# The last row of a hybrid layer stack made as two units of 256 tokens, with gate and output products in parts

## What is computed

```python
x = x + _L0_attn_a_ref(_layernorm(x), ...)   # mamba block
x = x + _L0_ffn_ref(_layernorm(x), ...)      # ternary FFN "a"
x = x + _L0_attn_b_ref(_layernorm(x), ...)   # minGRU
x = x + _L0_ffn_ref(_layernorm(x), ...)      # ternary FFN "d"
```

```python
def step(hstate, inp):
    dt_s, B_s, C_s, u_s = inp
    dA = jnp.exp(dt_s[..., None] * A)
    hstate = dA * hstate + (dt_s * u_s)[..., None] * B_s[:, None, :]
    y = jnp.einsum('bdn,bn->bd', hstate, C_s)
    return (hstate, y)
```

## Time and profile before

| | |
|---|---|
| median of three runs | 849.01 us (847.75 to 850.52) |
| the profiled execution | 847.88 us |
| its span in the trace | 846.1 us (1.8 us lie outside) |
| mean granted TensorE clock | 0.905 of full |
| first scan of row 0; of row 7 | 34.04 us; 645.91 us |
| end of the last scan step (row 7) | 731.9 us |
| from there to the end of the span | 114.2 us |

### The profile page before, as it was taken

One profiled execution on the slowest core, in us unless ns is written; L12 is line 12 of the kernel. 1 busy time (PEld: TensorE's weight loads), 2 busy tenths in 40 slices (PEclk: granted clock), 3 DMA queues, 4 the chain that ended last, 5 costly groups with the idle time before them and its releaser, 6 DMA issues. The chain is left out here.

```text
span 846.1 us, 12506 instructions
## 1 busy us (share of the span) xinstructions
PE 704.9 (83%) x4060; PEld 592.6 (70%) x4060; DVE 677.5 (80%) x1063; ACT 638.3 (75%) x965; POOL 586.3 (69%) x375
## 2 busy tenths in 40 slices
PE   5666576799689988899789979999789968988966
PEld 4454465588677876688667868688668857877765
DVE  4799988799977997999888998799879987743131
ACT  5787877896899878987999688987896588335312
POOL 3499768777768787978777887878796578225312
PEclk9678577999899997999899989999899989998995
DMA  5511211111111211121111211211112110000000
GB/s 140 175 62 63 76 51 54 48 64 51 38 51 52 63 38 58 44 72 42 52 45 56 63 39 52 63 51 48 53 32 71 50 51 26 0 1 2 13 1 12
DMA packets 35185, 42.79 MB, mean 51 GB/s; under 512 B 7457, under 2 KB 17074, under 8 KB 35122
## 3 DMA queue, kind: packets, MB, share of 16 engines
q1 hardware_dynamic: 35122, 42.00, 16.3%
HBM read 39.63 MB, written 2.36 MB: 50 GB/s over the span
## 5 line engine op out<-in xcount | busy, mean ns | idle before, releaser
L523 POOL TENSOR_TENSOR inflow<-dtu,b_all 128x1024 f32<-128x1024 f32 x127 | 308.9, 2435 | 72.3 <-DVE state L1127 45.9
L1127 DVE TENSOR_TENSOR_SCAN state<-dA,inflow 128x512 f32<-128x512 f32 x256 | 298.4, 1207 | 27.1 <-ACT dA L874 23.9
L874 ACT ACTIVATE dA<-dt,decay_c 128x512 f32<-128x512 f32 x256 | 170.1, 686 | 48.2 <-DVE state L1127 47.2
L1144 DVE TENSOR_TENSOR state<-state,c_ps 128x1024 f32<-128x1024 f32 x128 | 155.7, 1216 | 18.8 <-PE c_ps L1432 13.9
L1441 PE MATMUL y_ps<-ident,state 128*128 128x128 f32 x1024 | 149.9, 295 | 0.0
L1441 PEld LDWEIGHTS y_ps<-ident,state 128*128 128x128 f32 x1024 | 134.6, 154 | 13.8 <-issue 4.1
L1432 PE MATMUL c_ps<-xd,pick 128*128 128x512 f32 x128 | 64.2, 502 | 58.0 <-DVE state L1144 57.3
L1325 PE MATMUL work<-in_hi,wzh_hi 128*128 128x512 f32 x256 | 104.2, 407 | 2.3 <-POOL in_lo L685 2.2
L1326 PE MATMUL work<-in_hi,wzh_lo 128*128 128x512 f32 x256 | 101.0, 395 | 0.0
L1327 PE MATMUL work<-in_lo,wzh_hi 128*128 128x512 f32 x256 | 101.0, 394 | 0.0
L676 POOL TENSOR_TENSOR wide<-wide 128x512 f32<-128x512 f32 x48 | 61.2, 1274 | 29.0 <-ACT wide L921 26.8
(11 more groups left out here) (172 smaller groups left out, 1491.4 us busy)
## 6 DMA issues: line engine op xcount, KB each, us to landing
b_all<-b_scratch SPq DMA_DIRECT2D x128, 256.0 KB, 3.1
x_tok<-in_x SPq DMA_DIRECT2D x8, 256.0 KB, 3.8
out_x<-x_tok SPq DMA_DIRECT2D x8, 256.0 KB, 3.7
wide<-in_Wz SPq DMA_DIRECT2D x1, 1024.0 KB, 7.9
wide<-in_Wh SPq DMA_DIRECT2D x1, 1024.0 KB, 8.3
skip_f<-in_W SPq DMA_DIRECT2D x2, 256.0 KB, 4.1
dtu<-in_W_in SPq DMA_DIRECT2D x1, 256.0 KB
mixed<-in_w_up SPq DMA_DIRECT2D x1, 256.0 KB, 2.8
```

Of the source, the lines that this page charges most:

```text
L523: eng.tensor_tensor(inflow[:, n % 2, :, tok(b)], dtu[:, :, tok(b)], b_all[:, n % RING, tok(b)].unsqueeze(1).broadcast_to([P, HALVES, TO[b] ...
L874: act.activation(dA[:, h, tok(b)], dt[:, b % 2, h, tok(b)], ACT.Exp, scale=decay_c[:, h, n:n + 1]).then_inc(s_dA[h], 1)
L1127: dve.tensor_tensor_scan(state[:, g % 3, h, tok(b)], dA[:, h, tok(b)], inflow[:, n % 2, h, tok(b)], first, ALU.mult, ALU.add).then_inc(s_s ...
L1144: dve.tensor_tensor(state[:, g % 3, :, tok(b)], state[:, g % 3, :, tok(b)], c_ps[:, tok(b)].unsqueeze(1).broadcast_to([P, HALVES, TO[b] - ...
```

## The change

Row 7 becomes two units. The first (called **A** here, tokens 0 to 255) starts at slot 112, where row 7 started. The second (**B**, tokens 256 to 511) starts at slot 128. Each goes through all stages at 256 columns. While A is scanned its last state column is copied into `carry` after each step (16 copies), and B's scans start from there. Gate products may now be issued in two parts (input blocks 0 and 1, then 2 and 3), the skip and `mixed` matmuls of `out` block by block. 24 `keep_clock` matmuls stand ahead of the last unit's norm 3 and 4 ahead of its first FFN d product. The order tables are set anew for all rows (among others: the splitting of the gate weights in row 0 is moved by up to 5.5 slots, and the bank table has some entries swapped).

```diff
 UNITS = (
-    (0, 0, 512, 0), ..., (6, 0, 512, 96), (7, 0, 512, 112),
+    (0, 0, 512, 0), ..., (6, 0, 512, 96), (7, 0, 256, 112), (7, 256, 512, 128),
 )
...
-    "splitzh2": 9, "splitzh3": 10.5,
+    "splitzh2": 10.5, "splitzh3": 16,
...
+            WARM = {3: 24}
...
             def norm_t(t, m):
                 p = "norm%d" % m
+                if t == N - 1 and m in WARM:
+                    keep_clock(WARM[m])
...
             def ffn_up(t, c, j):
                 p = c + ".up%d" % j
+                if t == N - 1 and c == "d" and j == 0:
+                    keep_clock(4)
...
-            def gru_gate(t, which, j):
+            def gru_gate(t, which, j, part):
                 p = "%s%d" % (which, j)
-                pe.wait_ge(s_lozh, FB)
-                bank_free(t, p)
-                for k in range(FB):
+                if part == 0:
+                    pe.wait_ge(s_lozh, FB)
+                    bank_free(t, p)
+                for k in (2 * part, 2 * part + 1):
                     pe.wait_ge(s_inlo, FB * t + k + 1)
                     at = (which == "h") * FF + j * P
                     last = three(bank(p)[:, tok(t)], ...
-                last.then_inc(*made(p))
+                if part == 1:
+                    last.then_inc(*made(p))
...
-            def gru_out_skip(t):
-                bank_free(t, "out")
+            def gru_out_skip(t, k):
+                if k == 0:
+                    bank_free(t, "out")
...
-            def gru_out(t):
+            def gru_out(t, k):
```

More of the change, by code:

```diff
@@ L63 @@
     "d.gelu3": 40.75, "a.square3": 23, "d.square3": 41.25, "in3": 27, "in7": 27.5, "gate0": 30, "gate1": 31,
[1 row of a table removed]
[L65 removed]
[1 row of a table added]
+    "signs_t": 8.25,
 }
@@ new lines @@
+    ("ACT", "z_copy1", 1): -9, ("DVE", "a.ms", 1): 24.25, ("DVE", "dt", 1): -2, ("DVE", "factors3", 1): 38,
+    ("DVE", "gate", 1): 16.25, ("DVE", "hid1", 1): 34.25, ("DVE", "hid2", 1): 36.25, ("DVE", "hid3", 1): 36.25,
+    ("DVE", "lo2", 1): 27.25, ("DVE", "new0", 1): 31.25, ("DVE", "new1", 1): 32.5, ("DVE", "new3", 1): 35.25,
+    ("DVE", "norm", 1): -31.75, ("DVE", "read", 1): 0.5, ("DVE", "stats3", 1): 37.5, ("DVE", "x1", 1): 17.5,
[11 rows of a table added]
+    ("POOL", "base", 1): -2.5, ("POOL", "conv1", 1): -11.75, ("POOL", "conv2", 1): -10.75,
[3 rows of a table added]
@@ new lines @@
+    ("DVE", "factors1", 7): 18.25, ("DVE", "factors3", 7): 39.5, ("DVE", "gate", 7): 13.25,
+    ("DVE", "hid0", 7): 33.75, ("DVE", "hid1", 7): 33.75, ("DVE", "hid2", 7): 35.75, ("DVE", "lo1", 7): 19.25,
+    ("DVE", "lo2", 7): 29.75, ("DVE", "lo3", 7): 41.5, ("DVE", "new0", 7): 33.5, ("DVE", "new1", 7): 33.75,
+    ("DVE", "new3", 7): 36.25, ("DVE", "norm", 7): -19.5, ("DVE", "read", 7): 0.5, ("DVE", "scan", 7): 0.25,
+    ("DVE", "stats3", 7): 38.25, ("DVE", "x1", 7): 17.75, ("DVE", "x3", 7): 38.25, ("DVE", "xd_lo", 7): -9.75,
[15 rows of a table added]
@@ L241 @@
+    ("POOL", "conv2", 8): -12.75, ("POOL", "d.rms", 8): 47.5, ("POOL", "d.sum1", 8): 45.25,
+    ("POOL", "d.sum2", 8): 46.5, ("POOL", "d.sum3", 8): 46.5, ("POOL", "h_lo", 8): -16.25,
[3 rows of a table added]
+    ("POOL", "root", 8): -17.25, ("POOL", "x2b", 8): 31.25,
 }
@@ L1520, in gru_gate @@
                                  in_hi[:, k, tok(t)], in_lo[:, k, tok(t)], start=(k == 0), stop=(k == FB - 1))
[L1521 to L1540 removed]
+                if part == 1:
[3 more added lines that the diff above has]
+                    bank_free(t, "out")
+                evacuated(pe, t, "in%d" % (FB + k))
+                for j in tiles(t):
+                    pe.matmul(bank("out")[:, cols(j)], skip_f[:, k, cols(j)], wo_sb[:, k, :],
+                              start=(k == 0 and j == tiles(t)[0]), stop=False, skip_group_check=True)
+            def gru_out(t, k):
+                pe.wait_ge(s_hid, FB * t + k + 1)
+                for j in tiles(t):
+                    last = pe.matmul(bank("out")[:, cols(j)], mixed[:, k, cols(j)], wo_sb[:, k, :], start=False,
+                                     stop=(k == FB - 1), skip_group_check=True)
+                if k == FB - 1:
+                    last.then_inc(*made("out"))
             pe.wait_ge(s_const, 3)
@@ L1601, in _ @@
                         for t in due(r, s, PE_ON["%s%d" % (which, j)]):
-                            gru_gate(t, which, j)
-                for t in due(r, s, PE_ON["out"]):
-                    gru_out_skip(t)
-                for t in due(r, s, PE_ON["out+"]):
-                    gru_out(t)
+                            gru_gate(t, which, j, 0)
+                        for t in due(r, s, PE_ON["%s%d+" % (which, j)]):
+                            gru_gate(t, which, j, 1)
+                for k, p in enumerate(("out", "out+s1", "out+s2", "out+s3")):
+                    for t in due(r, s, PE_ON[p]):
+                        gru_out_skip(t, k)
+                for k, p in enumerate(("out+m0", "out+m1", "out+m2", "out+")):
+                    for t in due(r, s, PE_ON[p]):
+                        gru_out(t, k)
             assert all(begun[k] == len(SEQUENCE[k]) for k in range(BANKS))
```

141 lines of the change are left out of this document (65 added, 76 removed), and 247 rows, old and new, of tables (ACT_AT, BANK, DVE_AT, MOVED).

## The result

The changed kernel takes 878.33 us (median of four, 876.03 to 879.91) against 849.19 of the one before: a ratio of 1.034, 95% interval 1.033 to 1.036. It is slower by 29 us. The forecast was 856, so the direction was right and the size (7 us) a quarter of what came. The profiled execution took 876.03 us with a span of 874.2. It is the fastest of the four, 2.3 us under their median.

The account below looks back on a forecast made before the run. No engine alone bounds it; time is loose in a 114.2 us tail without scans. Span 645.9 - 3.5 + 51.3 + 28.0 + 46.0 + 85.3 = 853.0, plus 1.8 outside, 854.8; predicted 856, range 838 to 867.

Parts of the forecast that it names:

- Rows 0 to 6: Rows ahead of the halves: the new order cuts a quarter of the reads' 13.9 us of waits for C, -3.5 us.
- Tail, part (1): From B's last read to B's x1: 24 us, against 10.4 before.
- the clock falls: Rival: half-wide products idle TensorE more, lowering its clock in tail and pause; +11 us, 867; chance 0.10.
- A, B, and parts (2) to (4): A 51.3 us, B 46; tail from x1 to first `in` evacuation 23, to x3 20, to the end 18.3.
- the half step: One scan step at 256 columns: 1.96 us, plus 0.25 in A for the `carry` copy.
- Part (4): Tail from x3 to the end: 18.3 us against 28.2 before, with fillers keeping the clock.
- Parts (2) and (3): Tail from x1 to the first `in` evacuation, 23 us against 38.6; from there to x3, 20 against 37.1.
- The pause: Between A's last read and B's first scan: a chain with no scan step to cover it, 28.0 us.
- The fillers: keep_clock matmuls beside the last norm 3: hold TensorE's clock, worth 2.8 us, 1 us late at worst.
- The closed tail: Rival: two halves fill each other's waits, tail 76.8 us; with a pause of 25, 844.5 in all; chance 0.27.

Follow-up runs that it names:

- rows01_new: Kernel before, row 7 whole, with only rows 0 and 1 and the bank table in the changed order: 855.12 us, ratio 1.0066.
- split_old_rows_banks: Changed kernel with rows 0 to 4 in the old order and the whole bank table as before: 873.59 us, ratio 1.0300.
- a_tail_fillers: Changed kernel with keep_clock matmuls added ahead of row 6's d.up2 and A's third and fourth `in` products: 878.91 us, ratio 1.0334.
- b_silu_and_mixed_later: Changed kernel with B's silu of z and skip behind its first decay, row 6's first minGRU step behind B's first steps: 881.23 us, ratio 1.0352.
- no_fillers: Changed kernel without the 28 keep_clock matmuls of the end: 878.48 us, ratio 1.0339.

## Why the prediction was wrong

**Its sum failed at the step "Rows 0 to 6", -3.5 where 10.3 came.** I took the waits for C as something that a new order could only shorten, and gave no number to the other side. In these rows the reads' waits for C went from 12.5 us up to 14.8, and all waits of VectorE from 51.6 to 58.8. The lists could have shown it: VectorE asks for ms_a and x2 of row 1 half a slot earlier than before, and x1 of row 0 stands behind eight more transposes on TensorE. rows01_new measured 5.6 us for the order of rows 0 and 1 with its bank table. With rows 0 to 4 and the whole table as before some 4 us come back (split_old_rows_banks); with rows 0 and 1 alone nothing does. Which entries of the later rows cost the rest stays open.

**Tail, part (1), 24 where 30.6 came.** The list of the work ahead of B's x1 was right (24 `in` and 66 gate matmuls), its price was not: I had A's split matmuls at 0.116 and nothing between them, 10.4 us, and they took 15.8. A third of them ran at 0.21. The rival "the clock falls" was the one to price here, since the earlier trace rows already had 0.90 and 0.83 in the tail; I gave it 0.10 and put it nowhere in the sum. a_tail_fillers shows 2.8 us of the 6.6 as the clock's. The rest is read from the rows only: two waits of TensorE, longer first matmuls behind other work, and some 1.3 us more in the stretch ahead of A's `in` products and in the output product.

**A, B, and parts (2) to (4)** came within 1.8 us each. For the half step the reasoning held: A's steps with their copy take 2.27 us where nothing stands between (forecast 2.21), B's 2.05 to 2.09 (1.96; three halves of a fixed 0.07 on 1.78 make 1.99). Part (4) is luck. Its 18.3 had the fillers keep the clock, worth 2.8 us; they didn't, and it came to 18.5 with them and 18.6 without. Parts (2) and (3) fit this execution, 42.6 us together, and less well the seven traces that have 43.8 to 44.9.

**The pause** was missed by 2.0, and the link that was too short is x2 to the first `in` evacuation: 10.2 in the sum, 12.1 in the trace. The 10.2 came from row 7, with nothing in its way. In the pause the gelu and squares of row 5's FFN d and parts of B's preparation stand between on ScalarE, and norm 2's n_tok starts 4.4 us after VectorE made its variance (711.67 to 716.25). The same link is 13.8 us in split_old_rows_banks and makes its pause 31.7. Besides, row 6's first minGRU step on VectorE stands ahead of B's first scan in the list that the forecast itself shows, and I counted it as work that the pause covers. It ends last, 0.8 us behind the decay; b_silu_and_mixed_later shows the pause 2.7 us shorter with it and the silu moved.

**The fillers** were to be worth 2.8 us less 1 that they cost, and are worth nothing here (no_fillers). The cost was right, 0.9 us. They gain about as much in the up products and leave the way back at the lower clock.

**The rivals.** The closed tail was far off: 91.7, not 78. By its own sum TensorE stands 33.1 us of that (91.7 - 58.6), hardly less than the 36.4 of before, where the rival had 18.2. That this is because each half is one chain in one list is my reading and was not tested.

Of the 28 us by which the span grew, then, the pause with the half-wide steps is 40.3 (126.3 - 86.0), the rows ahead 10.3, and the tail gives back 22.5 (114.2 - 91.7). The forecast had 39.3, -3.5 and 28.9. That the scanned part would cost about 40 us and more than the tail gives back was right, and with it the direction.

## What to carry to other kernels

Splitting the last unit shortens the tail but asks for cover twice: here the tail gave back 22.5 us, and the scan of the second half began 30 us after the first had ended, since its preparation stood behind a stage of the row before. Price a link of such a chain with what stands beside it in the lists, not from a row that had nothing in its way. A new order is a cost with two signs; read in each list what is now asked for earlier, while its product is made no earlier, and price that. Where the rows show a serial tail at TensorE's lower clock, matmuls without a use in its waits are a cheap try (6 to 7 us here for 62 of them in six places, in the kernel before). Look for where a gain ends: in the changed kernel x1 came 2.8 us sooner and the time stayed the same.
